# Attention and a 64-expert layer on one core: second table cleared later, a fifth raw slot, three shared tiles stored by ScalarE

## The chip, the cores and the metric

The kernel runs on one core of one Trainium2 chip. The metric is the device time of one launch in microseconds; lower is better.

## The reference

Four batches of 512 tokens by 512 features go through an attention layer and then through a layer of 64 experts, everything in float32.

```python
# attention, per batch: layer norm, keys are the given context followed by new ones
q, k_new, v_new = xn @ wq.T, xn @ wk.T, xn @ wv.T
k, v = concat([ctx, k_new]), concat([ctx, v_new])
x = x + softmax(q @ k.T / sqrt(512)) @ v @ wo.T

# experts: 64 experts, the best 6 per token, at most 128 tokens each
scores = softmax(xf @ gate_w.T);  topk_w, topk_idx = top_k(scores, 6)
gu = einsum('ech,ehi->eci', xf[buf_tok], gate_up_proj)     # hidden width 192
eo = einsum('eci,eih->ech', silu(g) * u, down_proj) * buf_w
routed = zeros.at[buf_tok].add(eo)
shared = silu(xf @ shared_gate_w.T) * (xf @ shared_up_w.T) @ shared_down_w.T   # hidden width 384
x = x + routed + shared
```

## The kernel before, in words

Every float32 product is made of three TensorE matmuls on a high and a low part of each operand (`product`, lines 1189 to 1191). ScalarE (ACT) copies an operand to its high part, and VectorE (DVE) subtracts to get the low part.

**Two stages.** `attention_and_router` works through four batches b = 0 to 3. `experts` then runs 64 experts; its first instructions are woven into the last batch. Each stage has one program per engine, and the order of the work on each is written out by hand, with counting semaphores between them.

**Attention, on SyncE (`sync`, line 337).** SyncE issues nearly all loads and stores, in one queue. Before batch 0 it loads x and the first weights, stores zeros to the padding rows of the table, of `x2_rows` and of the output (lines 406 to 408), waits for these, and then clears `second_sum`, a table of 2048 + 128 rows of 512 in HBM, from the zero rows of `x2_rows` in two DMAs (lines 411 and 413). `body(b)` then loads `ctx`, the next x and `wo`, moves part of the transposed probabilities by small DMAs (`move_pair`, half by SyncE, half by ScalarE at line 324; the tile is `pT_lo<-res` in the trace), loads the next `ctxT'`, `wq'` and `wk'`, stores eight tiles of the batch's results (`out` at line 381, `x2_rows` at line 383), keeps `x2T` and loads `wv'`. TensorE then needs the moved pieces for its transposes at line 1005 and the products behind them. GpSimd (POOL) scatters the routing table.

**Experts.** Expert n's weights, gate, up and most of down, are one load of 1 MiB into `raw[n % 4]` (line 1369); the rest of down comes for two experts at once into one of two `rest` tiles (line 1373). A raw slot is free again when VectorE has split the down part of the expert in it. Loads 0 and 1 are issued inside the last batch, load 2 when its projection is done, load 3 and the later ones when `routed` is signalled (line 774), because slot 3 lies over memory of the attention stage. ScalarE and VectorE split the weights of expert e + 3 while TensorE works on expert e.

**Adding results.** The result rows of each expert, and of 12 of the 16 tiles of the shared part, go from PSUM through ScalarE (`out_rows`, line 1530) into one of six `eo` tiles, and from there with an adding indirect DMA by GpSimd into HBM (`add_rows`, line 1442). These 76 sets are numbered r = 0 to 75; even ones add to the output, odd ones to `second_sum`, and each waits until the one two before it has landed (line 1440). Before each GpSimd may gather the rows of a later expert (line 1434). The first three sets are the shared tiles (0, 0), (0, 1) and (0, 2). The sum at the end (`merge`, line 1471) adds `second_sum` to the output; four shared tiles of batch 2 are added by VectorE and stored plainly by SyncE (line 1417).

Of the kernel before, what the change touches and what calls it, by code (L numbers as in the profile page):

```python
# [102 lines left out]
def attention_and_router(nc, ctx, sem, t, table, x2_rows, second_sum, x2T_kept, kept):  # L103
# [232 lines left out]

    def sync(sp, before_last_rows):
# [16 lines left out]
        def body(b, more):  # L354
            load_item(b, more, "ctx", b)
            if more:

                if b:
                    sp.wait_ge(chosen_ready, b)
                    sp.wait_ge(router_exp, b * 2 * NT)  # L360
                else:
                    sp.wait_ge(group_taken, place(0, "first", ("xnT", NT - 1)) + 1 + BANKS)
                for a in range(QUADS):
                    sp.dma_start(xn[a * SQ:(a + 1) * SQ, :, :], x_quads[b + 1, a]).then_inc(x_loaded, 16)
            load_item(b, more, "wo")

            move_pair(sp, b, 0, 2)
            sp.wait_ge(pair_moved, (b + 1) * 16 * QUADS * QUADS)
            sp.dma_start(res[:, :, :], x_v[b]).then_inc(res_loaded, 16)
            if more:  # L370
                load_item(b, more, "ctxT'", b + 1)
                move_xnT(sp, b, 0, 2)
                for name in ("wq'", "wk'"):
                    load_item(b, more, name, b + 1)
            if not more:
                for name in ("sg", "su", "sd"):
                    load_item(b, more, name)
                before_last_rows(sp)
            for i in range(NT):
                sp.wait_ge(base_ready, b * NT + i + 1)  # L380
                sp.dma_start(out_v[b, i], res[:, i, :]).then_inc(base_stored, 16)
                sp.wait_ge(x2_ready, b * NT + i + 1)
                sp.dma_start(x2_v[b, i], x2[:, i, :]).then_inc(x2_stored, 16)
            if more:

                sp.wait_ge(group_taken, place(b, more, ("x2T", NT - 1)) + 1 + BANKS)
                for n in range(2):
                    sp.dma_start(x2T_kept[b, n], plain(x2T[n].rearrange("p c n -> p (c n)"))
                                 ).then_inc(x2T_stored, 16)
                load_item(b, more, "wv'")  # L390
# [9 lines left out]
        for name in FIRST_ITEMS[1:]:  # L400
# [8 lines left out]
        sp.wait_ge(pads_stored, 48)  # L409
        zeros = x2_rows[T:ROWS, :]  # L410
        sp.dma_start(second_sum[0:T, :].rearrange("(n p) d -> n p d", p=P),
                     zeros.unsqueeze(0).to_broadcast([T // P, P, D])).then_inc(kept.sum_cleared, 16)
        sp.dma_start(second_sum[T:ROWS, :], zeros).then_inc(kept.sum_cleared, 16)
# [783 lines left out]
RAW = 4  # L1197
# [55 lines left out]
CHAINED = len(SETS)  # L1253
SETS += [("shared", tile) for tile in TILES_OF[LAST]]
# [12 lines left out]
def experts(nc, ctx, sem, t, table, x2_rows, second_sum, x2T_kept, kept):  # L1267
# [10 lines left out]
    rest = [sb(f"rest{n}", [P, D]) for n in range(2)]  # L1278
# [10 lines left out]
    raw.append(sb("raw3", [P, ROW]))  # L1289
# [29 lines left out]
    rest_loaded = [sem(f"rest_loaded{n}") for n in range(2)]  # L1319
# [25 lines left out]
    tiles_stored = sem("tiles_stored")  # L1345
    last_rows_added = sem("last_rows_added")
# [19 lines left out]
    def load_weights(sp, n):  # L1366
        if n >= RAW:
            sp.wait_ge(weights_split, PIECE_NO["dn", n - RAW, 0] + 1)
        sp.dma_start(raw[n % RAW][:, :], t["expert"][n], max_dma_last_dim=4096).then_inc(raw_loaded[n % RAW], 16)
        if n % 2 == 0:  # L1370
            if n >= 4:
                sp.wait_ge(weights_split, PIECE_NO["dn", n - 3, 0] + 1)
            sp.dma_start(rest[n // 2 % 2][:, :], t["rest"][n // 2]).then_inc(rest_loaded[n // 2 % 2], 16)
# [19 lines left out]
    def sync(sp):  # L1393

        sp.wait_ge(kept.group_full, kept.projected)
        load_weights(sp, 2)

# [4 lines left out]
        for n in range(3, 7):  # L1402
            load_weights(sp, n)
        for e in range(E):
            if e + 7 < E:
                load_weights(sp, e + 7)
# [16 lines left out]
    def gpsimd(pool):  # L1423
# [13 lines left out]
        def add_rows(what):  # L1437
            r = SET_NO[what]
            if r >= 2:
                pool.wait_ge(added[r % 2], r // 2 * 16)  # L1440
# [14 lines left out]
        pool.wait_ge(kept.sum_cleared, 32)  # L1455
        gather(3)
        add_rows(("shared", (0, 0)))
        for e in range(4, 7):
            gather(e)
        add_rows(("shared", (0, 1)))  # L1460
        gather(7)
        gather(8)
        add_rows(("shared", (0, 2)))
# [10 lines left out]
        for n in range(2):  # L1474
            pool.wait_ge(added[n], CHAINED // 2 * 16)
# [10 lines left out]
    def act_weights(act, first, past):  # L1486
        for kind, n, part in PIECES[first:past]:
# [3 lines left out]
            else:  # L1491
                hi, (own_rows, _) = dn[n % DN_SLOTS][0], rest_rows(n)
                act.activation(hi[:, 0:D], raw[n % RAW][:, GU:ROW], ACT.Copy)  # L1493
                act.wait_ge(rest_loaded[n // 2 % 2], n // 4 * 16 + 16)
                act.activation(hi[own_rows, D:2 * D], rest[n // 2 % 2][own_rows, :], ACT.Copy).then_inc(weights_high, 1)  # L1495
# [19 lines left out]
    def scalar(act):  # L1515
# [8 lines left out]
        def out_rows(what):  # L1524
            r = SET_NO[what]
            act.wait_ge(dn_full, r + 1)
            if r >= EO:
                act.wait_ge(added[r % 2], ((r - EO) // 2 + 1) * 16)
# [3 lines left out]
        out_rows(("shared", (0, 0)))  # L1532
        out_rows(("shared", (0, 1)))
# [10 lines left out]
        out_rows(("shared", (0, 2)))  # L1544
# [31 lines left out]
    def dve_weights(dve, first, past):  # L1576
        for kind, n, part in PIECES[first:past]:
# [4 lines left out]
            else:  # L1582
                (hi, lo), (own_rows, other_rows) = dn[n % DN_SLOTS], rest_rows(n)
                subtract(dve, lo[:, :], raw[n % RAW][:, GU:ROW], hi[:, 0:D])
                subtract(dve, hi[other_rows, D:2 * D], rest[n // 2 % 2][own_rows, :],
# [217 lines left out]
def build(nc, t):  # L1803
# [4 lines left out]
    with ExitStack() as ctx:  # L1808
# [9 lines left out]
        kept.idx_all = ctx.enter_context(nc.sbuf_tensor("idx_all", [P, E + T // P], I32))  # L1818
        kept.tab_loaded = sem("tab_loaded")
# [74 lines left out]
```

## Time and profile before

| | us |
|---|---|
| median of 3 runs | 797.64 (796.4 to 797.65) |
| the profiled execution, its own time | 801.92 |
| span of its trace | 800.2 |
| PE busy in the span | 758.1 (95%) |
| DVE, ACT, POOL busy | 604.1, 449.7, 318.5 |
| attention stage (PE never long idle) | about 0 to 400 |
| expert stage | about 400 to 771 |
| end: last tiles and sum | 771 to 800.2 |

All times below are microseconds from the start of the span. A row of the timeline shows start, duration, engine, line, operation, output and inputs, and in brackets how long the engine had been idle before it and what ended that. The DMA share is the mean share of the 16 DMA engines' time that packets took; with two queues at work it can pass 1.

### The profile page before, as it was taken

Reading aid. Unit: us, or ns where it says so; the run is one execution under the profiler, and the core shown is the slowest. Engines: PE = TensorE matmul, PEld = TensorE weight load, DVE = VectorE, ACT = ScalarE, POOL = GpSimd, SP = SyncE. Lnnn points to the kernel's source line nnn. Section 1 sums busy time; section 2 is a strip of 40 time slices with the busy share of each in tenths; the row PEclk is TensorE's granted clock in tenths of the full one; section 3 lists DMA queues with packets and bytes.
Section 4 is the critical chain, followed back from the end, with each engine's and each line's share of the span. In section 5 each row is a group of like instructions: output and inputs, shape, how many; then the busy total and the mean of one; then the engine's idle time right before and its main releaser. Section 6 shows DMA issues by size and latency. Waiting matters only on the chain.

```text
span 800.2 us, 10843 instructions
## 1 busy us (share of the span) xinstructions
PE 758.1 (95%) x3774; PEld 640.8 (80%) x3774; DVE 604.1 (75%) x1191; ACT 449.7 (56%) x795; POOL 318.5 (40%) x256
## 2 busy tenths in 40 slices
PE   6998999999999999999999999999999999998972
PEld 5886877878888787888788789998888898887752
DVE  6545575895768866785577899999999999998622
ACT  3425323253332433344153899999899898988610
POOL 1000010348104351055315556556666577555530
PEclk9999999999999999999999999999999999999997
DMA  4895435545436356343466999999999999999888
GB/s 164 292 239 142 126 138 210 131 133 159 190 126 159 107 170 242 113 95 130 169 231 179 318 349 349 350 357 354 344 356 344 350 347 355 343 352 339 212 178 190
DMA packets 84757, 188.75 MB, mean 236 GB/s; under 512 B 26000, under 2 KB 32528, under 8 KB 81040
## 3 DMA queue, kind: packets, MB, share of 16 engines
q1 hardware_dynamic: 53488, 143.41, 49.8%
q0 software_dynamic: 19056, 40.98, 22.1%
q10 hardware_dynamic: 12160, 3.67, 2.3%
q8 instruction: 31, 0.51, 0.3%
q14 instruction: 22, 0.18, 0.1%
HBM read 144.38 MB, written 43.92 MB: 235 GB/s over the span
## 4 chain that ended last, share of the span: by engine, by line
PE 59%; DMA 12%; DVE 7%; issue 6%; POOL 6%; ACT 5%; ACTq 2%; SPq 0%; POOLq 0%; DVEq 0%
PE bank L1189 9%; PE bank L1191 9%; PE bank L1190 9%; DMA raw<-expert_in 7%; PE ps_gu L1189 3%; PE scores L1189 3%; PE ps_gu L1191 3%; PE ps_gu L1190 3%; PE scores L1191 3%; PE scores L1190 3%; POOL second_sum L1442 2%; POOL out_rows L1442 2%; PE bank L1005 2%; DVE gu_lo L1574 2%; PE bank L1168 1%
## 5 line engine op out<-in xcount | busy, mean ns | idle before, releaser
L480 POOL DMA_INDIRECT table<-rows,slot x72 | 84.7, 1177 | 145.0 <-DVEq L929 112.7
L1574 DVE TENSOR_TENSOR gu_lo<-raw,gu_hi 128x768 fp32r<-128x768 f32 x126 | 120.1, 955 | 14.2 <-ACT gu_hi L1490 13.2
L1490 ACT ACTIVATE gu_hi<-raw 128x768 fp32r<-128x768 f32 x128 | 107.3, 841 | 7.4 <-DMA raw<-expert_in 7.3
L1189 PE MATMUL ps_gu<-gu_hi,xgT_hi 128*128 128x384 f32 x256 | 91.8, 358 | 0.0
L1191 PE MATMUL ps_gu<-gu_hi,xgT_lo 128*128 128x384 f32 x256 | 86.8, 339 | 0.0
L1190 PE MATMUL ps_gu<-gu_lo,xgT_hi 128*128 128x384 f32 x256 | 86.5, 338 | 0.0
L508 ACT ACTIVATE qT<-bank 128x512 fp32r<-128x512 f32 x32 | 19.1, 597 | 109.1 <-PE bank L1191 78.1
L1434 POOL DMA_INDIRECT xg<-x_rows,idx_all x39 | 46.7, 1198 | 42.2 <-DVEq L750 17.4
L1442 POOL DMA_INDIRECT out_rows<-product,idx_all x25 | 44.4, 1774 | 36.5 <-DMA out_rows<-product,idx_all 17.3
L513 ACT ACTIVATE pbuf<-scores,negmax 128x1024 f32<-128x1024 f32 x16 | 17.8, 1113 | 65.2 <-DVE negmax L679 48.4
L651 DVE TENSOR_TENSOR qT<-bank,qT 128x512 fp32r<-128x512 f32 x32 | 22.0, 688 | 41.2 <-ACT qT L508 41.2
L1190 PEld LDWEIGHTS ps_gu<-gu_lo,xgT_hi 128*128 128x128 f32 x256 | 48.6, 190 | 0.0
L1189 PEld LDWEIGHTS ps_gu<-gu_hi,xgT_hi 128*128 128x128 f32 x256 | 48.4, 189 | 0.0
L1191 PEld LDWEIGHTS ps_gu<-gu_hi,xgT_lo 128*128 128x128 f32 x256 | 48.4, 189 | 0.0
L1574 DVE TENSOR_TENSOR dn_lo<-raw,dn_hi 128x512 fp32r<-128x512 f32 x64 | 43.9, 687 | 2.5 <-ACT dn_hi L1495 1.9
L1574 DVE TENSOR_TENSOR dn_hi<-rest,dn_hi 64x512 fp32r<-64x512 f32 x64 | 43.9, 687 | 0.9
L1189 PE MATMUL bank<-xnT_hi,w_hi 128*128 128x512 f32 x112 | 44.2, 395 | 0.0
L1574 DVE TENSOR_TENSOR xgT_lo<-ps_xgT,xgT_hi 128x512 fp32r<-128x512 f32 x64 | 43.8, 684 | 0.2 <-ACT xgT_hi L1509 0.2
L1191 PE MATMUL bank<-xnT_hi,w_lo 128*128 128x512 f32 x112 | 43.7, 390 | 0.0
L1190 PE MATMUL bank<-xnT_lo,w_hi 128*128 128x512 f32 x112 | 43.6, 389 | 0.0
L1493 ACT ACTIVATE dn_hi<-raw 128x512 fp32r<-128x512 f32 x64 | 40.5, 633 | 2.7 <-DVEq L774 2.7
L644 DVE TENSOR_TENSOR w_lo<-stage,w_hi 128x2048 fp32r<-128x2048 f32 x16 | 36.5, 2289 | 7.1 <-ACT w_hi L500 7.0
(293 smaller groups left out, 2214.3 us busy)
## 6 DMA issues: line engine op xcount, KB each, us to landing
raw<-expert_in SPq DMA_DIRECT2D x64, 1024.0 KB, 13.4
rest<-rest_in SPq DMA_DIRECT2D x32, 256.0 KB, 9.9
x_rows<-pbuf SPq DMA_DIRECT2D x17, 256.0 KB, 2.1
xn<-x_in SPq DMA_DIRECT2D x16, 256.0 KB, 5.0
stage<-wkT_in SPq DMA_DIRECT2D x4, 1024.0 KB, 4.9
stage<-ctxT_in SPq DMA_DIRECT2D x4, 1024.0 KB, 7.4
stage<-wvT_in SPq DMA_DIRECT2D x4, 1024.0 KB, 9.0
stage<-ctx_in SPq DMA_DIRECT2D x4, 1024.0 KB, 10.3
```

Of the source, the lines that this page charges most:

```text
L480: pool.indirect_dma_start(out=table, out_offset=bass.IndirectOffsetOnAxis(ap=slot[:, i, k:k + 1], axis=0), in_=rows[:, i, k, :], in_offset ...
L508: act.activation(split_dest(group)[0], split_source(key, group), ACT.Copy).then_inc(high_done, 1)
L644: dve.tensor_tensor(lo, item_stage(key, name), hi.bitcast(F32), ALU.subtract).then_inc(item_low, 1)
L651: dve.tensor_tensor(lo, split_source(key, group), hi.bitcast(F32), ALU.subtract).then_inc(group_taken, 1)
L1189: pe.matmul(out, still[0], moving[0], start=first, stop=False)
L1190: pe.matmul(out, still[0], moving[1], start=False, stop=False)
L1191: return pe.matmul(out, still[1], moving[0], start=False, stop=last)
L1434: pool.indirect_dma_start(out=xg[e % XG], out_offset=None, in_=x2_rows, in_offset=index(("expert", e))).then_inc(gathered[e % XG], 16)
L1442: pool.indirect_dma_start(out=(t["out"], second_sum)[r % 2], out_offset=index(what), in_=eo[r % EO], in_offset=None, compute_op=ALU.add).t ...
L1490: act.activation(gu[n % GU_SLOTS][0][part], gate_up_of(n, part), ACT.Copy).then_inc(weights_high, 1)
L1493: act.activation(hi[:, 0:D], raw[n % RAW][:, GU:ROW], ACT.Copy)
L1574: return dve.tensor_tensor(lo, x, hi.bitcast(F32), ALU.subtract)
```

## The change

The clearing of `second_sum` leaves the start of SyncE's program. It is done in `body(1)` and `body(2)`, behind the load of `wk'`: in batch 1 the 128 padding rows and tiles 3 to 7, in batch 2 tiles 8 to 15. Tiles 0 to 2 are not cleared. Instead the first three shared tiles are stored plainly into them by ScalarE, each right behind its `out_rows`. GpSimd adds these three no more; it waits once for the three stores before its loop over the experts, and the sets from r = 3 on are chained as before. `raw` has five slots and `rest` three. The new `raw3` and `rest2` lie in memory that both stages keep, so load 3 is issued with load 2, ahead of `routed`; `raw4` takes the place of the old `raw3`. The room comes from the reserve for GpSimd's DMA descriptors, which is set to 4096 bytes per partition.

```diff
+    def clear_sum(sp, b):
+        zeros = x2_rows[T:ROWS, :]
+        if b == 1:
+            sp.wait_ge(pads_stored, 48)
+            sp.dma_start(second_sum[T:ROWS, :], zeros).then_inc(kept.sum_cleared, 16)
+        half = T // P // 2
+        first = LEAD_TILES if b == 1 else half
+        sp.dma_start(second_sum[first * P:b * half * P, :].rearrange("(n p) d -> n p d", p=P),
+                     zeros.unsqueeze(0).to_broadcast([b * half - first, P, D])).then_inc(kept.sum_cleared, 16)
...
                 for name in ("wq'", "wk'"):
                     load_item(b, more, name, b + 1)
+                if b:
+                    clear_sum(sp, b)
...
-        sp.wait_ge(pads_stored, 48)
-        zeros = x2_rows[T:ROWS, :]
-        sp.dma_start(second_sum[0:T, :].rearrange("(n p) d -> n p d", p=P),
-                     zeros.unsqueeze(0).to_broadcast([T // P, P, D])).then_inc(kept.sum_cleared, 16)
-        sp.dma_start(second_sum[T:ROWS, :], zeros).then_inc(kept.sum_cleared, 16)
...
-RAW = 4
+RAW = 5
+REST = 3
...
+def added_before(r):
+    return len(range(LEAD_TILES + (r - LEAD_TILES) % 2, r, 2)) * 16
...
-    raw.append(sb("raw3", [P, ROW]))
+    raw.append(kept.raw3)
+    raw.append(sb("raw4", [P, ROW]))
...
-            if n >= 4:
-                sp.wait_ge(weights_split, PIECE_NO["dn", n - 3, 0] + 1)
-            sp.dma_start(rest[n // 2 % 2][:, :], t["rest"][n // 2]).then_inc(rest_loaded[n // 2 % 2], 16)
+            if n >= 2 * REST:
+                sp.wait_ge(weights_split, PIECE_NO["dn", n - 2 * REST + 1, 0] + 1)
+            sp.dma_start(rest[n // 2 % REST][:, :], t["rest"][n // 2]).then_inc(rest_loaded[n // 2 % REST], 16)
...
         sp.wait_ge(kept.group_full, kept.projected)
         load_weights(sp, 2)
+        load_weights(sp, 3)
...
         sp.wait_ge(kept.routed, 1)
-        for n in range(3, 7):
+        for n in range(4, E):
             load_weights(sp, n)
-        for e in range(E):
-            if e + 7 < E:
-                load_weights(sp, e + 7)
...
-            if r >= 2:
-                pool.wait_ge(added[r % 2], r // 2 * 16)
+            if r >= LEAD_TILES + 2:
+                pool.wait_ge(added[r % 2], added_before(r))
...
-        pool.wait_ge(kept.sum_cleared, 32)
-        gather(3)
-        add_rows(("shared", (0, 0)))
-        for e in range(4, 7):
+        pool.wait_ge(kept.sum_cleared, 48)
+        for e in range(3, 9):
             gather(e)
-        add_rows(("shared", (0, 1)))
-        gather(7)
-        gather(8)
-        add_rows(("shared", (0, 2)))
+        pool.wait_ge(lead_stored, LEAD_TILES * 16)
         for e in range(E):
             gather(e + 9)
...
-        out_rows(("shared", (0, 0)))
-        out_rows(("shared", (0, 1)))
+        def lead_rows(i):
+            out_rows(("shared", (0, i)))
+            act.wait_ge(eo_ready, i + 1)
+            act.dma_start(second_sum[i * P:(i + 1) * P, :], eo[i]).then_inc(lead_stored, 16)
+
+        lead_rows(0)
+        lead_rows(1)
...
-        out_rows(("shared", (0, 2)))
+        lead_rows(2)
...
-    nc = bacc.Bacc("TRN2", target_bir_lowering=False, num_devices=1)
+    nc = bacc.Bacc("TRN2", target_bir_lowering=False, num_devices=1, dynamic_dma_scratch_size=4096)
```

## Rows read from the trace of the kernel before

**Rows 1.** The page: granted clock and DMA share, 40 slices of 20 us.
```profile
PEclk9999999999999999999999999999999999999997
DMA  4895435545436356343466999999999999999888
```

**Rows 2.** Timeline of PE: its waits for the moved pieces, batches 0 and 2.
```profile
71.40 1.58 PE L1005 MATMUL bank<-ident,pbuf 128*128 128x128 f32 x8 [3.57 <-DVE v_lo L651]
...
264.88 1.16 PE L1005 MATMUL bank<-ident,pbuf 128*128 128x128 f32 x8 [0.33 <-DVE v_lo L651]
```

**Rows 3.** Chain that ended last: start, duration, the moved pieces landing, batches 0 and 2.
```profile
60.58 6.16 DMA pT_lo<-res
...
256.58 3.65 DMA pT_lo<-res
```

**Rows 4.** DMA issues of 31 to 37 us: queue, count, KB each, us to landing.
```profile
stage<-ctx_in SPq DMA_DIRECT2D x1, 1024.0 KB, 19.1
...
second_sum<-x_rows SPq DMA_DIRECT2D x1, 15.7
```

**Rows 5.** Windows: length, busy PE, PEld, DVE, ACT, POOL, granted clock, DMA share, GB/s.
```profile
32.00:55.00 23.00, 23.00 (x104) 19.02 (x103) 9.56 (x12) 6.11 (x9) 0.00 (x0) 1.00 0.97 282
...
70.00:75.00 5.00, 3.60 (x14) 3.03 (x15) 4.40 (x8) 3.19 (x7) 0.00 (x0) 0.70 0.80 321
```

**Rows 6.** Timeline of SP, batch 1: the load ahead of the new clears, the one behind.
```profile
192.83 0.33 SPq L352 DMA_DIRECT2D stage<-wkT_in  x1
...
216.10 0.93 SPq L352 DMA_DIRECT2D stage<-wvT_in  x1
```

**Rows 7.** Timeline of ACT, batch 1: the use of that load.
```profile
225.11 1.92 ACT L500 ACTIVATE w_hi<-stage 128x2048 fp32r<-128x2048 f32 x1 [5.25 <-DMA stage<-wvT_in]
```

**Rows 8.** Timelines of DVE and PE, batch 1: the routing sums, PE's product behind them.
```profile
239.35 1.00 DVE L900 TENSOR_TENSOR earlier<-earlier,xn 128x64 bf16<-128x64 bf16 x4
...
241.37 0.20 PE L1143 MATMUL bank<-chosen_b,before 128*128 128x64 bf16 x1
```

**Rows 9.** Windows of the expert stage, columns as in the fifth group.
```profile
480.00:540.00 60.00, 60.00 (x337) 54.15 (x336) 58.88 (x104) 55.42 (x104) 35.13 (x27) 1.00 1.06 352
540.00:735.00 195.00, 188.76 (x1031) 166.74 (x1030) 180.72 (x319) 175.76 (x326) 123.18 (x81) 0.99 1.06 348
```

**Rows 10.** DMA issues of 480 to 540 us.
```profile
raw<-expert_in SPq DMA_DIRECT2D x13, 1024.0 KB, 12.8
...
out_rows<-product,idx_all POOLq DMA_INDIRECT x4, 8.3
```

**Rows 11.** DMA issues of 600 to 660 us.
```profile
raw<-expert_in SPq DMA_DIRECT2D x12, 1024.0 KB, 13.8
...
out_rows<-product,idx_all POOLq DMA_INDIRECT x5, 8.8
```

**Rows 12.** Timeline of POOL: adds r = 3, 23, 70, 75, and the first load behind.
```profile
453.39 1.58 POOL L1442 DMA_INDIRECT second_sum<-eo,idx_all  x1 [0.30 <-issue]
...
545.62 1.78 POOL L1442 DMA_INDIRECT second_sum<-eo_above,idx_all  x1 [2.20 <-DMA second_sum<-eo,idx_all]
...
753.50 1.55 POOL L1442 DMA_INDIRECT out_rows<-product,idx_all  x1 [2.11 <-DMA out_rows<-eo,idx_all]
...
765.96 1.55 POOL L1442 DMA_INDIRECT second_sum<-eo,idx_all  x1 [0.79 <-DMA second_sum<-product,idx_all]
771.58 0.86 POOL L1478 DMA_DIRECT2D raw<-second_sum  x1 [4.07 <-DMA second_sum<-eo,idx_all]
```

**Rows 13.** Timeline of ACT: where the three stores go, and the last result tile.
```profile
437.44 0.33 ACT L1522 ACTIVATE silu<-ps_gu 128x192 f32<-128x192 f32 x1 [1.51 <-PE ps_gu L1191]
...
447.57 0.60 ACT L1530 ACTIVATE eo<-ps_dn 128x512 f32<-128x512 f32 x1 [0.24 <-PE ps_dn L1191]
...
755.99 0.69 ACT L1530 ACTIVATE eo<-ps_dn,tab 128x512 f32<-128x512 f32 x1 [1.57 <-PE ps_dn L1752]
```

**Rows 14.** Chain that ended last: start and duration of one DMA issue on ACT.
```profile
58.57 0.64 ACTq L324
```

More of the change, by code:

```diff
@@ L1277, in experts @@
     raw = [sb(f"raw{n}", [P, ROW]) for n in range(2)]
-    rest = [sb(f"rest{n}", [P, D]) for n in range(2)]
+    rest = [sb(f"rest{n}", [P, D]) for n in range(2)] + [kept.rest2]
     gu = [(halves(sb("gu_hi0", [P, GU], F32R)), halves(sb("gu_lo0", [P, GU], F32R)))]
@@ L1318, in experts @@
     raw_loaded = [sem(f"raw_loaded{n}") for n in range(RAW)]
-    rest_loaded = [sem(f"rest_loaded{n}") for n in range(2)]
+    rest_loaded = [sem(f"rest_loaded{n}") for n in range(REST)]
     gathered = [sem(f"gathered{n}") for n in range(XG)]
@@ L1345, in experts @@
     tiles_stored = sem("tiles_stored")
+    lead_stored = sem("lead_stored")
     last_rows_added = sem("last_rows_added")
@@ L1474, in gpsimd @@
         for n in range(2):
-            pool.wait_ge(added[n], CHAINED // 2 * 16)
+            pool.wait_ge(added[n], added_before(CHAINED + n))
         pool.nop().then_inc(chains_done, 1)
@@ L1493, in act_weights @@
                 act.activation(hi[:, 0:D], raw[n % RAW][:, GU:ROW], ACT.Copy)
-                act.wait_ge(rest_loaded[n // 2 % 2], n // 4 * 16 + 16)
-                act.activation(hi[own_rows, D:2 * D], rest[n // 2 % 2][own_rows, :], ACT.Copy).then_inc(weights_high, 1)
+                act.wait_ge(rest_loaded[n // 2 % REST], n // 2 // REST * 16 + 16)
+                act.activation(hi[own_rows, D:2 * D], rest[n // 2 % REST][own_rows, :], ACT.Copy).then_inc(weights_high, 1)
     def act_silu(act, n):
@@ L1526, in out_rows @@
             act.wait_ge(dn_full, r + 1)
-            if r >= EO:
-                act.wait_ge(added[r % 2], ((r - EO) // 2 + 1) * 16)
+            if r >= EO + LEAD_TILES:
+                act.wait_ge(added[r % 2], added_before(r - EO + 2))
+            elif r >= EO:
+                act.wait_ge(lead_stored, LEAD_TILES * 16)
             scale = tab[:, what[1], 1:2] if what[0] == "expert" else 1.0
             act.activation(eo[r % EO], ps_dn[:, r % 2, :], ACT.Copy, scale=scale).then_inc(eo_ready, 1)
-        out_rows(("shared", (0, 0)))
-        out_rows(("shared", (0, 1)))
+        def lead_rows(i):
[4 more added lines that the diff above has]
+        lead_rows(1)
         gate(0)
@@ L1584, in dve_weights @@
                 subtract(dve, lo[:, :], raw[n % RAW][:, GU:ROW], hi[:, 0:D])
-                subtract(dve, hi[other_rows, D:2 * D], rest[n // 2 % 2][own_rows, :],
+                subtract(dve, hi[other_rows, D:2 * D], rest[n // 2 % REST][own_rows, :],
                          hi[own_rows, D:2 * D]).then_inc(weights_split, 1)
@@ L1818, in build @@
         kept.idx_all = ctx.enter_context(nc.sbuf_tensor("idx_all", [P, E + T // P], I32))
+        kept.raw3 = ctx.enter_context(nc.sbuf_tensor("raw3", [P, ROW], F32))
+        kept.rest2 = ctx.enter_context(nc.sbuf_tensor("rest2", [P, D], F32))
         kept.tab_loaded = sem("tab_loaded")
```

## The prediction

> **What bounds the kernel now.** I read the slices of the page first [rows 1]. The DMA share has two full stretches, 20 to 60 us and everything from 440 us on; between them the DMA engines are half idle. Up to 440 us TensorE (PE) runs nearly without a gap, so that stage costs what its matmuls cost, plus PE's few waits. The longest by far is in batch 0: 3.57 us before the transposes at 71.40. The same transposes in batch 2 waited 0.33 us [rows 2]. In both the chain of waits runs through the small moves `pT_lo<-res`: behind ScalarE's last issue they took 6.16 us in batch 0 and 3.65 us in batch 2 [rows 3]. The work is the same; what differs is the queue. The clearing DMA took 15.7 us to land, and the `ctx` load behind it 19.1 us [rows 4]. [...]
>
> The expert stage has three limits close together. From 480 to 540 us PE is busy 60.00 of 60.00 us and DVE 58.88; from 540 to 735 us PE is busy 188.76 of 195, so 6.24 us are idle [rows 9]. The DMA share is 1.06 and the rate 348 to 352 GB/s in both. The third limit is the chain of adds. Add r = 23 starts at 545.62 and r = 70 at 753.50, 47 steps of 4.42 us; each waits for the add two before it. After the loads, r = 70 to 75 take 5 steps of 2.49 us [rows 12]. The last result tile is started at 755.99 and ready at 756.68 [rows 13], yet its add goes out at 765.96, 9.3 us later. So at the end the adds are last, not the matmuls and not the loads. At 771.58 the final sum begins; the 28.6 us from there to the end of the span are not changed.
>
> **The change part by part.**
>
> *Clear taken out of the start.* It removes 17 tiles of 256 KiB, 4.46 MB. At 282 GB/s [rows 5] that is 15.8 us, which agrees with the landing of 15.7 us [rows 4]. With `ctx`, x and `wo` (3.15 MB) the queue holds 7.6 MB from 32 us on, 27 us of work, so it is full until about 59 us, when the moves are being issued. Without the clear it is empty after 11 us, near 43 us. Then batch 0 should look like batch 2: PE waits 0.33 instead of 3.57 us, a gain of 3.24 us. The lower bound is the difference of the moves alone, 2.51 us [rows 3]. [...] All of this is on PE's path, and PE has no slack behind it until 440 us, so it reaches the expert stage whole. Sum: -4.7 us (-2.5 to -4.7).
>
> *Clear put into batches 1 and 2.* It goes behind the `wk'` load, near 193 us in batch 1 [rows 6]; the queue is half idle there [rows 1]. Queued behind it on SyncE's ring are eight stores of results, the two of `x2T` and the `wv'` load at 216.10. Spread over all engines the larger part, 8 tiles or 2.1 MB, takes 7.4 us at 282 GB/s and is over before 216. Then it costs nothing. If it lasts longer, `wv'` lands late. ScalarE already waits 5.25 us for it [rows 7]; behind it DVE finishes the routing sums at 240.35, 1.0 us before PE's product that needs them [rows 8]. The upper bound is that the new clear takes as long as the old one, 15.7 us [rows 4]: from about 198 to 213.7 us, then 2.1 MB of stores, 7.4 us, so the two of `x2T` and `wv'` run some 5.5 us late, and less the 1.0 us PE waits 4.5 us in each of two batches. I take 0.3 us (0 to +9), near the lower end, because 2.1 MB at the rate used above are done before 216.
>
> What the rows show of spreading is one DMA of 16 tiles in 15.7 us [rows 4]. [...]
>
> *Fifth raw slot, third rest slot.* Load 3, 1.05 MB, moves from 441 us to near 402 us, where the DMA share is 0.6 [rows 1], so it is hidden. It is gone from the full stretch: 1.05 MB at 348 GB/s, 3.0 us. Every later load is issued one expert earlier. That can fill PE's 6.24 idle us [rows 9], but this is worth nothing while the adds are last. What remains is that the loads end 3.0 us earlier, and that the adds go from 4.42 to 2.49 us a step 3.0 us earlier: 3.0 x (1 - 2.49 / 4.42) = 1.3 us. Bounds: 0, and all of the 6.2 us. I take -1.3.
>
> *Three adds less, three stores more.* Two stores are issued by ScalarE before the `silu` at 437.44, which waited 1.51 us for PE [rows 13]; an issue is 0.64 us [rows 14], 1.28 for both, so they are covered. The third comes behind `out_rows` at 447.57, where ScalarE is otherwise full: 0.64 us, part of it on the path. GpSimd waits for its landing before `gather(9)` and the add r = 3. Landing as an add did, 8.3 us [rows 10], from 448.8, that is 457; then a gather, so r = 3 goes out near 458.5 instead of 453.39 [rows 12]. Queued behind are the later gathers (needed six experts later, no cost) and the chain. From r = 3 to 23 the steps were 4.61 us; the chain can do 4.42, so 20 steps regain 3.8 of the 5.1 us, and all of it if landings are shorter there. What is left at r = 23 is 0 to 1.3 us. Both items together: +0.4 us (0 to +2).
>
> *Smaller descriptor reserve.* At no time are more than a few DMAs of GpSimd open (two adds, up to five gathers), so I cost it at nothing; GpSimd's issue durations of 1.55 to 1.78 us [rows 12] would show it.
>
> Sum: -4.7 + 0.3 - 1.3 + 0.4 = -5.3 us. The profiled execution took 801.92 us with a span of 800.2, 4.3 us above the median of 797.64. Nothing in the sum scales with that, so the profiled time becomes 796.6 and the median 792.3 us.
>
> **The rivals.**
>
> 1. *The loads were the limit after all.* If the adds speed up once ScalarE and the loads no longer collide with them, the whole 6.2 us of PE's idle time go instead of 1.3: 797.64 - 4.7 + 0.3 + 0.4 - 6.2 = 787.4 us. For it: PE has no idle time at all up to 540 us and 6.24 us after it. Against it: the 9.3 us by which the adds trail. Chance 0.12.
>
> 2. *The moved clears hold `wv'` up.* If one engine copies one tile, five or eight tiles take as long as sixteen did, and the stores and `wv'` wait in the same rings. Half of the 5.5 us, less the 1.0 us, is 1.8 us in each of two batches: +3.6 instead of +0.3, 795.6 us. For it: everything of the batch's end is queued behind the clear. Against it: the 5.25 us of ScalarE's wait are hidden today, and part of DVE's work behind has gaps. Chance 0.18. [...]
>
> 3. *Slower: the deeper load queue lengthens the adds.* With five slots SyncE has one more load open all the time. Between 480 to 540 and 600 to 660 us the landing of loads rose from 12.8 to 13.8 us and that of the adds from 8.3 to 8.8 [rows 10, 11]: more open loads, slower adds. Another open load (about +4.4 us of landing) could add several times as much. Each us of landing is 0.5 us a step; over 52 adds from r = 23 it takes +0.27 us of landing to eat up 7 us, which turns -5.3 into +1.7. With the +0.5 us that the rows show once more, the price is 52 x 0.25 = 13 us, 805.3 us; with half of it, 798.8 us, which I give as its time. Against it: when adds are late, the six result tiles run out, ScalarE stops and with it the loads, so the queue empties again. Chance 0.10.
>
> 4. *The clear did not cause the wait of batch 0.* The x load shares the queue too. Then only the fifth slot gains: 797.64 + 0.3 - 1.3 + 0.4 = 797.0 us. Against it: 3.15 MB are 11 us of work, gone long before the moves. Chance 0.06.
>
> **How the numbers follow.** The forecast, 792.3 us, has 0.54, with a range of its own of 789.5 to 795. Below it lies rival 1, above it rivals 2, 4 and 3. The range from 786.5 to 798 takes in rivals 1, 2 and 4, and leaves out rival 3 and the far ends of 2. About 0.2% (1.6 us) is what a measurement of this kernel can tell from no change, so faster means below 796.0: the forecast, rival 1 and two thirds of rival 2, 0.78. Same: rival 4 and most of what is left of rival 2, 0.11. Slower: rival 3 and its like, 0.11.
>
> **What would show it.** In the trace after: PE's wait before the transposes of batch 0 near 0.3 us and a full clock behind it; the first wait for `routed` about 5 us earlier, near 436 us; ScalarE's waits for expert loads gone; the steps of the adds still about 4.4 us while loads run, and the last add about 5 us earlier, near 760.5. The landing of `wv'` in batches 1 and 2 against 9 us decides rival 2, that of the adds rival 3. The prediction is wrong if the adds' landing moves by more than 0.3 us either way, since 52 of them stand in one chain.

## The result, and the profile after

The changed kernel takes 804.68 us (median of 7 runs, 802.0 to 805.72), the kernel before 797.65 beside it. The ratio is 1.0068, 95% interval 1.0041 to 1.0095: slower, where 792.3 us was forecast. The profiled execution of the changed kernel took 802.37 us, with a span of 800.5. It lies 2.3 us under its median and that of the kernel before 4.3 us over its own, so the two traces end almost together (0.3 us apart in their spans) where the medians are 7.0 us apart; what the change costs as a whole is read from the medians, and where it costs from the traces.

The page, granted clock and DMA share, answers to [rows 1]. The windows (columns as in [rows 5] and [rows 9]) show batch 0's wait and the same stage of batches 1 and 2:

```profile
PEclk9999999999899999999999999999999999999997
DMA  5833552636536375524295899999999999999888
...
60.00:80.00 20.00, 19.85 (x94) 16.03 (x94) 18.03 (x32) 9.61 (x17) 1.02 (x1) 1.00 0.33 112
200.00:220.00 20.00, 15.72 (x67) 12.35 (x66) 12.13 (x21) 6.59 (x9) 2.75 (x4) 0.83 0.50 193
300.00:320.00 20.00, 16.03 (x70) 12.75 (x70) 12.10 (x21) 5.88 (x8) 2.74 (x4) 0.91 0.52 205
```

The first window is what was forecast: where PE waited 3.57 us [rows 2] and ran at a clock of 0.70 [rows 5], it is busy 19.85 of 20 us at full clock. The other two are new. PE is busy only 15.72 and 16.03 us, at a granted clock of 0.83 and 0.91: it was 0.50 from 208 to 214 us in batch 1 and from 314 to 316 us in batch 2. PE's timeline in batch 1 has two waits ahead of the transposes of x2, which stretch from 207.77 us on:

```profile
207.77 1.09 PE L1013 MATMUL bank<-ident,pbuf 128*128 128x128 f32 x4 [1.83 <-DVEq L852]
...
211.09 1.94 PE L1013 MATMUL bank<-ident,pbuf 128*128 128x128 f32 x8 [2.23 <-DVE qT L659]
```

The waits of 190 to 225 us say who was late (us in total, times, longest), and the chain of waits through the same stretch (start, duration, what) gives the order:

```profile
POOL rstd L474 <- DMA table<-rows,slot: 11.4, 1, 11.4
DVE pbuf L794 <- POOL rstd L474: 6.6, 2, 6.1
...
190.94 12.17 DMA table<-rows,slot
203.28 0.58 POOL rstd L474
203.89 0.55 DVE pbuf L794
204.44 0.67 DVE res L849
```

GpSimd's last scatter of batch 0's routing table was issued at 190.94 us and landed 12.17 us later. GpSimd waits for all scatters before it goes on to the norms (`rstd`) of batch 1; VectorE waits 6.1 us for the first norm, and PE for VectorE's `pbuf`. In the kernel before, GpSimd has no wait for scatters there at all, only for VectorE:

```profile
POOL rstd L466 <- DVE veps L848: 6.3, 4, 1.7
```

What lay in the way is the moved clear. The packet records of the changed kernel show 20 packets of 64 KiB in batch 1 (five tiles, on five engines, 191.9 to 202.2 us) and 32 in batch 2 (on eight engines, 293.2 to 303.8 us): five and eight at a time, four times behind each other, 2.42 to 3.00 us each. The last scatter landed at 203.1 us, 0.9 us after the last of them had gone. In batch 2 GpSimd waited 10.6 us. The same records show how a few bytes come to wait so long. The packets of GpSimd's queue (64 bytes or less) take 0.013 us each in the median; in batch 1 exactly five of them start at 194.42 to 194.92 us, five at 196.85 to 197.34 and five at 199.27 to 199.76, each time where the five large ones change over, and the rest from 201.70 on. Batch 2 shows the same with eight (295.88 to 296.28, 298.36 to 298.70, 300.78 to 301.12). So in both batches each busy engine started one small packet between two of its large ones, 15 in batch 1 and 24 in batch 2 over the three changeovers, and the scatters' last packets followed as the large ones ended.

**The ledger.** PE issues the same 3774 matmuls in the same order in every kernel here, so the start of the same matmul can be compared. Rows are points of the program (start in the kernel before), columns the difference to that kernel in us. The labels are those of the experiments below. All columns stand against one execution of the kernel before, the one that took 4.3 us more than its median. e4 ran on a chip that no other column here is from, where e1 to e4 all show further short waits of 1.0 to 1.6 us (near 165, 194, 292 and 362 us, in e4 some 8 us later) that the other chips don't; of its column only the steps from row to row are used, not the level.

```
before   after  e4      e6     e9     e12    e8     e11    e10
 67.4    -1.0   -0.0    +0.5   -0.1   +0.5   -1.3   +0.3   -0.4   ahead of batch 0's wait
 77.7    -5.8   +2.7    -4.3   -4.9   -4.4   -6.2   -4.4   -5.1   behind it
199.1    -6.4   +5.8    -4.8   -5.3   -5.1   -6.7   -4.9   -5.6   batch 1, ahead of the norms
225.7    +0.0   +5.8    -4.8   -5.3   -4.9   -6.7   -4.9   -5.6   behind them
318.7    +5.7   +7.5    -4.7   -5.3   -4.8   -6.5   -5.0   -5.5   batch 2, behind the norms
421.0    +5.3  +11.3    -4.7   -5.4   -5.1   -6.9   -5.6   -5.5   last batch
459.6    +5.3   +9.7    -6.3   -7.0   -6.8   -8.4   -7.2   -7.2   experts begin
588.1    +4.1   +8.5    -7.5   -8.3   -7.9   -7.2   -8.4   -8.4
661.9    +3.3   +7.6    -8.3   -8.9   -8.8   -5.9   -9.3   -8.1
750.9    +2.1   +8.2    -8.3   -7.8  -10.2   -6.2   -8.3   -8.0
```

The changed kernel wins 4.8 us at batch 0's wait and loses 6.4 and 5.7 us behind the norms of batches 1 and 2. e5, the changed kernel once more, loses 6.7 and 6.6 us at the same two places (-5.3 at 199.1, +1.4 at 225.7, +8.0 at 318.7). In the expert stage the profiled execution regains 3.2 us, and ScalarE's waits for expert loads, 7.3 us before, are down to 0.7. The 3.2 us are no steady gain: e5 has none of these waits either and stands at +7.8 at 459.6, +5.9 at 661.9 and +8.8 at 750.9. The adds hold the end as before [rows 12], now at

```profile
L1500 ACT ACTIVATE gu_hi<-raw 128x768 fp32r<-128x768 f32 x128 | 107.3, 841 | 0.7 <-DMA raw<-expert_in 0.7
...
460.14 1.63 POOL L1457 DMA_INDIRECT second_sum<-eo,idx_all  x1 [0.30 <-issue]
...
550.60 1.98 POOL L1457 DMA_INDIRECT second_sum<-eo_above,idx_all  x1 [2.00 <-DMA second_sum<-eo,idx_all]
...
755.37 1.55 POOL L1457 DMA_INDIRECT out_rows<-product,idx_all  x1 [1.23 <-DMA out_rows<-eo,idx_all]
...
767.81 1.55 POOL L1457 DMA_INDIRECT second_sum<-eo,idx_all  x1 [0.53 <-DMA second_sum<-product,idx_all]
773.51 0.87 POOL L1488 DMA_DIRECT2D raw<-second_sum  x1 [4.15 <-DMA second_sum<-eo,idx_all]
```

(the first row is ScalarE's group of weight copies: busy, mean ns, and at its end the idle time before them; the others are the adds r = 3, 23, 70 and 75 and the load behind).

From that last load to the end of the span it was 28.6 us before and is 27.0 now. Nearly all of the difference is in one instruction, with which GpSimd ends its program (in the kernel before and in the changed one: line, instruction, count, duration in ns as least/median/most, start):

```profile
L1823 POOLq DRAIN  x1: 2602/2602/2602, 797.4 to 797.4; - x1
```

```profile
L1842 POOLq DRAIN  x1: 1173/1173/1173, 799.1 to 799.1; - x1
```

It takes 2602 ns in the kernel before and in e8, and 1173 ns in all twelve traces with the reserve of 4096 bytes. So 1.43 us of the span go with the change. The reserve is the part of the change that all twelve have and these two lack, next to the place of the new tiles in memory; no run changes it alone, so it is the likely cause and not a shown one.

### The profile page after: what moved, and what is told of

Same layout as the page of the kernel before. It is cut to its first block, busy times and chain, and to the rows that moved or that the text cites. A ratio compares the mean times of both kernels' runs of the same rounds, so it can differ in the third digit from the quotient of the medians.

```text
span 800.5 us, 10842 instructions
## 1 busy us (share of the span) xinstructions
PE 758.5 (95%) x3774; PEld 640.1 (80%) x3774; DVE 603.6 (75%) x1191; ACT 449.4 (56%) x795; POOL 310.1 (39%) x253
## 4 chain that ended last, share of the span: by engine, by line
PE 69%; DMA 10%; DVE 6%; POOL 5%; issue 5%; ACT 3%; SPq 1%; POOLq 0%; DVEq 0%
PE bank L1197 9%; PE bank L1199 9%; PE bank L1198 9%; PE ps_gu L1197 4%; PE ps_gu L1199 4%; PE ps_gu L1198 4%; PE scores L1197 3%; PE scores L1199 3%; PE scores L1198 3%; DMA table<-rows,slot 3%; PE ps_dn L1197 2%; PE ps_dn L1199 2%; PE ps_dn L1198 2%; PE ps_xgT L1727 2%; DMA out_rows<-product,idx_all 2%
## 5 line engine op out<-in xcount | busy, mean ns | idle before, releaser
L1591 DVE TENSOR_TENSOR gu_lo<-raw,gu_hi 128x768 fp32r<-128x768 f32 x126 | 120.2, 955 | 11.4 <-ACT gu_hi L1500 10.4
L1457 POOL DMA_INDIRECT out_rows<-product,idx_all x24 | 41.0, 1707 | 27.4 <-DMA out_rows<-product,idx_all 14.9
```

Source lines behind the costliest of these rows:

```text
L1457: pool.indirect_dma_start(out=(t["out"], second_sum)[r % 2], out_offset=index(what), in_=eo[r % EO], in_offset=None, compute_op=ALU.add).t ...
L1591: return dve.tensor_tensor(lo, x, hi.bitcast(F32), ALU.subtract)
```

## The experiments

The experiments went to three chips; the kernel before took 807.85, 798.74 and 797.61 us (medians) beside the first four, the next four and the last four. So all is compared by the ratio to the kernel before on the same chip.

**Is it the clears, and what about them?** e1 writes the same bytes with the 128 rows of a tile outermost, in packets of 2 KiB, by its records mostly 15 to 17 at a time while the clear runs:

```diff
-        sp.dma_start(second_sum[...].rearrange("(n p) d -> n p d", p=P),
-                     zeros.unsqueeze(0).to_broadcast([b * half - first, P, D]))
+        sp.dma_start(second_sum[...].rearrange("(p n) d -> p n d", p=P),
+                     zeros.unsqueeze(1).to_broadcast([P, b * half - first, D]))
```

> The changed kernel, with each clear of the second table laid out over 128 partitions' worth of rows (outermost dimension 128, rows of 2 KB) instead of 5 or 8 whole tiles. Theory H (held scatters): GpSimd's table scatters share DMA engines with packets of 64 KiB, each of about 2.4 us; GpSimd waits for all of them before it may compute the next norms, and so TensorE waits in batches 1 and 2 and its clock falls. Then the last scatter lands within about 3 us, both waits (6.4 and 5.7 us with the clock) are gone: 804.7 - 12 = 792.7 us. Rival S (stores and wv' late behind the clear): the bytes are the same and the queue is the same, so at most the part from the five and eight busy engines goes; little change, 803 to 805 us. Rival M (memory traffic of the clears slows everything around it): no change, 804.7 us.

Measured: 800.41 us, ratio 0.9903 (0.988 to 0.9925). GpSimd's wait is 4.6 us in batch 1 and 5.8 in batch 2 (theory H had the last scatter land within 3 us), and PE's waits ahead of the transposes of x2 are down to 0.2 us. Spreading changed two things at once, the engines and the packets. e2 leaves the shape and only limits the packets:

```diff
-                     zeros.unsqueeze(0).to_broadcast([b * half - first, P, D]))
+                     zeros.unsqueeze(0).to_broadcast([b * half - first, P, D]), max_dma_last_dim=512)
```

> The changed kernel with the clears still over 5 and 8 whole tiles, but cut into packets of 2 KB instead of 64 KiB. H with packet size as the cause: a scatter waits for one small packet at a time, the waits in batches 1 and 2 go as with the spread layout, 793 us. H with the few engines as the cause (what counts is that five or eight engines are busy for 10 us): the waits stay, 804.7 us. S: 804.7 us, since the clears hold the same rings for as long.

Measured: 799.09 us, ratio 0.9884 (0.9862 to 0.9907), GpSimd's wait 4.5 us. The limit counts bytes here: the packets are 512 bytes long, not the 2 KiB that the expectations say of this and of the later kernels with the limit. The queue's row of the page (packets, MB, share) has 6604 more than the changed kernel, 13 tiles in 512 bytes less the 52 large ones. By the records most of the time five to seven of them are under way together in batch 1 (193.6 to 205.9 us) and eight to twelve in batch 2 (290.1 to 302.7 us), against 15 to 17 in e1. So a clear on few engines did no harm by itself. The short packets have a price of their own, though it is hidden: SyncE's next store is held at its issue for 5.50 us in e2 and 7.50 in e9, against 0.34 to 0.35 in the changed kernel, e1 and e12, and PE does not wait longer for that. e9 is the same kernel on the third chip (0.9914); these are the changed kernel's row and its own:

```profile
q1 hardware_dynamic: 53473, 142.62, 49.2%
```

```profile
q1 hardware_dynamic: 60077, 142.62, 50.0%
```

e12 goes the other way: long packets, but on all 16 engines.

```diff
-        sp.dma_start(second_sum[...].rearrange("(n p) d -> n p d", p=P),
-                     zeros.unsqueeze(0).to_broadcast([b * half - first, P, D]))
+        count = (b * half - first) * P // 16
+        sp.dma_start(second_sum[...].rearrange("(p m) d -> p (m d)", p=16),
+                     zeros[0:count, :].rearrange("m d -> (m d)").unsqueeze(0).to_broadcast([16, count * D]))
```

> The changed kernel with each moved clear written as 16 long rows (80 KiB in batch 1, 128 KiB in batch 2), so that all 16 DMA engines take part with packets as large as before. Theory Q (a large packet ahead in a DMA engine holds GpSimd's small scatters by its own length, and the number of packets in each engine decides: four each in the changed kernel, one or two here): GpSimd's wait for the table's scatters 6 to 9 us, less than 1.5 us of waiting by TensorE in batches 1 and 2 together, ratio 0.992 to 0.998. Theory S (any packet of such size costs the same stop, whatever the number): GpSimd's wait stays at 10 to 12 us and the ratio at 1.003 to 1.008. Theory O (even so, the spread takes the harm away entirely): wait under 5.5 us, ratio as e9.

Measured: 790.28 us, ratio 0.9912 (0.9889 to 0.9935). By its records the rows were cut in two, 32 packets of 40 KiB in batch 1 and 32 of 64 KiB in batch 2, 16 at a time and so two on each engine, one of 64 KiB 2.42 to 2.84 us. GpSimd's and VectorE's waits, first batch 1, then batch 2 (windows 190 to 225 and 290 to 325 us):

```profile
POOL rstd L476 <- DMA table<-rows,slot: 6.3, 1, 6.3
...
DVE pbuf L796 <- POOL rstd L476: 1.6, 2, 1.2
...
POOL rstd L476 <- DMA table<-rows,slot: 6.6, 1, 6.6
```

In batch 2 packets of exactly the changed kernel's size hold the scatters for 6.6 us when two stand on an engine and 10.6 us when four do; the difference, 4.0 us, is a little less than two packets of 2.42 us. This is theory Q. PE keeps its pace: its longest wait between 190 and 330 us is 0.4 us, so the norms had room for these 6.3 us. That the ratio is better than the forecast for Q fits this room.

**Is GpSimd's wait the whole path?** e3 and e6 leave the clears as they are and put the norms ahead of the wait.

```diff
             pool.tensor_tensor(rstd2[:, i:i + 1], ...).then_inc(rstd_ready, 1)
         if not more:
             return
+        if b:
+            pool.wait_ge(scattered, b * 16 * NT * K)
+            pool.sem_inc(slots_free, 1)
...
-        pool.wait_ge(scattered, (b + 1) * 16 * NT * K)
-        pool.sem_inc(slots_free, 1)
+        if b == B - 2:
+            pool.wait_ge(scattered, (b + 1) * 16 * NT * K)
+            pool.sem_inc(slots_free, 1)
```

This is e6. e3 had no exception for the last of these waits.

> The changed kernel with its clears untouched; only GpSimd's wait for its 24 scatters of a batch is moved behind the four norms of the next batch. H: the scatters still take about 12 us, but the norms no longer wait for them; both waits of TensorE go, 792.7 us. S and M: nothing that they name is changed, 804.7 us.

Measured: 812.38 us, ratio 1.0044 (1.0025 to 1.0063), a miss. The two waits were gone, but a new one came in the last batch (PE's timeline):

```profile
410.36 0.76 PE L1198 MATMUL ps_gu<-v_hi,kT_hi 128*128 128x512 f32 x1 [10.41 <-DMA v_lo<-x2T_kept]
```

SyncE waits on `slots_free` before it loads the table and then `x2T`; the edit made that signal late. With the exception:

> The changed kernel with its clears untouched (64 KiB packets on 5 and 8 engines in batches 1 and 2), but GpSimd computes the next batch's norms before it waits for the scatters of batches 0 and 1; for batch 2, whose scatters the last batch's gathers need, the wait stays where it was. Theory H (held scatters: all that the moved clears cost is GpSimd's wait ahead of the norms): ratio about 0.989 (0.986 to 0.992), no wait of TensorE over 1.2 us between 190 and 330 us, and no 10 us wait near 410 us. Rival C (the clears also take bandwidth from what TensorE, ScalarE or VectorE wait for): some of the 1.8% stays, ratio 0.994 to 1.002, and waits for loads in batches 1 and 2 are seen in the trace.

Measured: 792.34 us, ratio 0.9925 (0.9899 to 0.9951), beside 1.0077 (1.0046 to 1.0107) for the changed kernel on the same chip:

> The changed kernel itself, on the chip of the runs of this call, as the measure for the others. Every theory: ratio to the kernel before 1.007 (1.003 to 1.010), GpSimd's rstd waiting 11 to 12 us for the table's scatters in batch 1 and 10 to 11 in batch 2.

The waits of 190 to 225 us show that GpSimd now waits for VectorE only, as in the kernel before:

```profile
POOL rstd L474 <- DVE veps L860: 8.8, 4, 4.0
```

From 199 to 319 us the ledger of e6 stands still (-4.8 to -4.7), with the large packets in the queues. So the two waits behind the norms cost 1.5% (about 12 us), and the clears cost PE nothing besides. Rival C falls. The medians of e5 and e6, 805.34 and 792.34 us, are 13.0 us apart, beside the 6.7 and 6.6 us that e5 lost at the two places.

**What is each part worth?** e8 is the kernel before with the clear moved and nothing else, in 512-byte packets.

> The kernel before with one thing changed: the clear of the second table goes out in batches 1 and 2 in 2 KiB packets and not at the start; four slots, GpSimd's adding scatters for the shared tiles. Theory S (the parts add up: slots and stores alone gave 0.56%, clear, slots and stores together 1.16%): ratio 0.994 (0.992 to 0.996), the 5 us won in batch 0 still there at the end. Theory P (the adds and loads of the experts' part soak up what the start gave): ratio 0.997 to 1.000, TensorE 5 to 6 us ahead at 400 us and less than 2 at 760. Theory L (slots and stores are worth nothing, once the clear is out of the way): 0.988 to 0.990.

Measured: 795.76 us, ratio 0.9969 (0.9946 to 0.9992). In the ledger 8.4 us are won by 460 us and 5.9 left at 662. The group of weight copies points to where it went:

```profile
L1499 ACT ACTIVATE gu_hi<-raw 128x768 fp32r<-128x768 f32 x128 | 107.3, 841 | 13.8 <-DMA raw<-expert_in 13.6
```

ScalarE's waits for loads grew from some 7 to 13.6 us: an expert stage that starts earlier, with four slots and the full DMA stretch unchanged, waits for its loads. The ratio is the one that theory P gives; the ledger of the profiled execution, with 6.2 us left at 751 us, is nearer to theory S. The medians (-3.0 us) leave less than that execution shows. Part of it is the slow execution that the ledger stands against (4.3 us over its median), part that this one took 794.59 us, 1.2 under its own. e4 does the opposite: slots and stores, but the 13 tiles cleared at the start.

> The changed kernel with the clear back at the start of SyncE's program (13 tiles and the padding rows), so fifth slot, third rest slot and ScalarE's stores alone. H: the waits of batches 1 and 2 go (-12 us) and that of batch 0 comes back (+4.8 us), and the expert stage keeps its gain of about 3 us: 797 us, a little under the kernel before (797.6 - 3 = 795). If the expert stage's gain was only the later start and not the slots: 797.6 us or more. S and M: the same as H here, since they too blame the clears of batches 1 and 2.

Measured: 803.99 us, ratio 0.9944 (0.9916 to 0.9971), better than H's 797 us (a ratio of 0.999). Batch 0's wait is back, longer than in [rows 2] (PE's timeline):

```profile
73.08 1.94 PE L1005 MATMUL bank<-ident,pbuf 128*128 128x128 f32 x8 [5.27 <-DVE v_lo L651]
```

e9, e10 and e11 take the slot and the stores apart, all with 512-byte clears. e10 (and e7 before it) has `RAW = 4` and `REST = 2`; e11 keeps five slots and gives the three shared tiles back to GpSimd.

```diff
-            act.wait_ge(eo_ready, i + 1)
-            act.dma_start(second_sum[i * P:(i + 1) * P, :], eo[i]).then_inc(lead_stored, 16)
...
-        for e in range(3, 9):
-            gather(e)
-        pool.wait_ge(lead_stored, LEAD_TILES * 16)
+        gather(3)
+        add_rows(("shared", (0, 0)))
...
```

> Clears in 2 KiB packets as in the second kernel of the first call, with four raw slots and two rest slots in place of five and three; the stores by ScalarE stay. Theory U (the fifth slot has a use, since ScalarE waited 7.3 us for loads with four): ratio 0.991 to 0.994, ScalarE's wait for raw loads back at 5 to 8 us. Theory N (the slot is hidden: TensorE and the adds end the kernel, ScalarE's waits for loads are slack): ratio 0.988 to 0.990 like with five slots, ScalarE's wait for loads back all the same. If four slots come out below 0.987, the deeper queue costs something by itself.

Measured: 792.86 us, ratio 0.993 (0.9907 to 0.9953), with 1.3 us of waiting for loads, not the 5 to 8 of theory U. e2 had been on another chip, so the comparison was made again on one:

> The changed kernel with the two moved clears in 2 KiB packets (e2_small again), now on one chip with its own four-slot and no-stores forms. Theory U (the fifth slot has a use of its own): ratio to the kernel before 0.989, 0.3% or more below e10. Theory N (the slot's work is hidden; e2 and e7 differed because they ran on two chips): ratio 0.991 to 0.993, within 0.2% of e10.

> The same with four raw slots and two rest slots (e7_small_four again). Both theories: ratio 0.993 (0.991 to 0.995), ScalarE's wait for raw loads 1 to 2 us.

> The changed kernel with its clears in 2 KiB packets and its five slots, but the first three shared tiles go by GpSimd's adding scatters as in the kernel before. Theory T (the stores carry the gain in the experts' part: with four slots, TensorE was 2.6 us further ahead at 588 us with stores than without, and ScalarE waited 1 us for loads and not 14): ratio 0.996 to 0.998, like e8, and ScalarE's waits for loads 5 us or more even with five slots. Theory D (slot or stores, either one removes ScalarE's waits for loads, and one is enough): ratio 0.990 to 0.993, within 0.2% of e9, waits for loads under 3 us.

Measured: e9 790.44 us, 0.9914 (0.9892 to 0.9937); e10 792.17 us, 0.9933 (0.9908 to 0.9958); e11 791.93 us, 0.9938 (0.9913 to 0.9962). The idle time of ScalarE's weight copies in e9, e10 and e11:

```profile
L1501 ACT ACTIVATE gu_hi<-raw 128x768 fp32r<-128x768 f32 x128 | 107.3, 841 | 0.0
```

```profile
L1501 ACT ACTIVATE gu_hi<-raw 128x768 fp32r<-128x768 f32 x128 | 107.2, 840 | 6.2 <-DMA raw<-expert_in 6.0
```

```profile
L1506 ACT ACTIVATE gu_hi<-raw 128x768 fp32r<-128x768 f32 x128 | 107.3, 841 | 3.4 <-DMA raw<-expert_in 3.3
```

The slot is worth 1.7 us and the stores 1.5 us by the medians. Both are small against the noise: the intervals overlap, and run against run five of e9's six times lie below all six of e11's, but only three of them below all of e10's. e9 against e10 is 0.19%, which is what theory N named; e10's 6.2 us of waits for loads are more than the 1 to 2 that both theories had. e11 lies just outside D on both counts (0.24% from e9, 3.4 us of waits) and farther from T.

Together (e9 at 0.9914 against e8 at 0.9969, two chips) it is 0.55% or 4.4 us, and e4 against the kernel before says the same, 0.56%. Both pairs hold the 1.43 us of GpSimd's last instruction too, so slot and stores have about 3.0 us of it, near 1.7 + 1.5.

The lowest times of this study are e12 and e9 (790.28 and 790.44 us); by the ratio e2, which is e9 on another chip, is lowest at 0.9884. All of them beat the kernel before and the changed one.

## Why the prediction was wrong

**Clear taken out of the start: right.** Forecast -4.7 us, measured -4.8 at the same place (67.4 to 77.7 in the ledger). Of the forecast, 3.24 us are the wait, and 1.5 us stand for the clock, 0.30 of the 5 us of [rows 5]; that share was the author's estimate, and no run shows it by itself. What the traces show is a clock of 0.50 from 72 to 75 us in the kernel before and of 1.00 there in the changed one. The wait and the lower clock behind it are gone, and with the clear back at the start (e4) the wait is back too. Rival 4 falls. About 1 us more stands ahead of it in the profiled pair (-1.0), but it differs from kernel to kernel with nothing changed there (-1.3 to +0.5) and is not put down to the change. What was too simple is that these 4.7 us go into the sum whole: e8, with this part alone and no harm in batches 1 and 2, has 0.9969, 2.5 us (0.6 to 4.3), and its ledger gives part of the gain back in the expert stage, where ScalarE waits 13.6 us for loads.

**Clear put into batches 1 and 2: the step that failed.** Forecast +0.3 us (0 to +9), measured +6.4 and +5.7, 12.1 us in all. The step named what is queued on SyncE behind the clear, the stores and `wv'`, and stopped there. It asked how long the clear lasts, and the upper bound even gave it the old 15.7 us, but not what else shares the DMA engines in that time. The last of GpSimd's 24 scatters of the batch before are on them, out of another queue (128 packets, started from 191.2 to 202.3 us in batch 1), and what stands behind them was to be found in the kernel: GpSimd waits for all of them and only then computes the norms that VectorE and PE need next. That wait is the missing term. Four large packets per engine (2.42 us each, 9.7 us) bound it from the trace after; what PE lost was less, because the norms had some room (5.2 us of such waiting in e9 cost nothing). The upper bound of the range, +9, also had a slip: 213.7 + 7.4 is 5.0 us past 216.1, not 5.5.

**Rival 2** had the layout right and the victim wrong. The large clears took 10.3 and 10.6 us, not the old one's time. `wv'` landed 9.0 us after its issue, as in the kernel before (DMA issues of 199 to 221 us: queue, count, KB, us to landing):

```profile
stage<-wvT_in SPq DMA_DIRECT2D x1, 1024.0 KB, 9.0
```

e6 shows that it was not issued late either: with the large packets in the queues and only the norms moved it goes out at 211.34 us, 4.8 us before the 216.10 of [rows 6], which is all that this kernel is ahead by then.

```profile
211.34 0.91 SPq L363 DMA_DIRECT2D stage<-wvT_in  x1
```

That one engine copies one tile fits the trace, five and eight large packets at a time. By itself this cost nothing: e2 keeps the shape and is among the fastest (0.9884). The harm came with the large packets: at each changeover of five or eight of them five or eight small ones start, and in e12, with two large packets on an engine (of 40 KiB in batch 1) in place of four, GpSimd waits 6.3 and 6.6 us for the scatters and not 11.4 and 10.6.

**Fifth slot: the size about right, the reason only in part.** Forecast -1.3 us, measured -1.7 (e9 against e10) with an uncertainty of the same size. ScalarE's waits for loads went, as forecast; that the loads end 3.0 us earlier and the adds speed up for it was not measured by itself.

**Stores for adds: probably the wrong sign.** Forecast +0.4 us, measured -1.5 by the medians, not certain. The first add (r = 3 at 460.14) came less late than forecast, which was 458.5, or 463.8 with the 5.3 us by which everything was late there. That three adds less make room in the full DMA stretch fits ScalarE's waits for loads (3.4 us in e11, none in e9), but isn't shown beyond that.

**Smaller reserve: a term put at nothing.** GpSimd's issues are as long as before (72 scatters at 1.18 us each in both), as the prediction said. But it also held the 28.6 us at the end for unchanged, and they are 27.0: 1.43 us less in GpSimd's last instruction.

**Rival 1 and rival 3.** The adds' steps from r = 23 to 70 became (755.37 - 550.60) / 47 = 4.36 us, from 4.42, and the landing of the group in [rows 11] went from 8.8 us to 8.4. That is past the 0.3 us that the prediction named as a sign of being wrong, but the other four groups of adds in that window moved by -0.4 to +0.2 and the same group has 8.9 in e9, so it is scatter and no deeper queue lengthened the chain. Loads land later, 16.0 us from 600 to 660 us instead of 13.8 (+2.2, where rival 3 had +4.4), and no harm is seen, since they are issued earlier. The last add came 9.0 us after its result tile, as before (6.6 in e9, 9.1 in e10), and PE's waits from 455 to 750 us are 6.5 us after 8.0 before (8.3 in e9), so rival 1's gain did not come either. The DMA issues of 600 to 660 us:

```profile
raw<-expert_in SPq DMA_DIRECT2D x12, 1024.0 KB, 16.0
...
out_rows<-product,idx_all POOLq DMA_INDIRECT x6, 8.4
```

**The sum.** Without the 12.1 us of the two waits the changed kernel's 804.68 us would be 792.6, and e9, the change as meant, has 0.9914 against the forecast's 792.3 / 797.64 = 0.9933. So near a hit is in part luck. Of e9's 6.9 us the clear has 2.5 and not 4.4 (-4.7 + 0.3), slot and stores 3.0 and not 0.9, and the end 1.4 and not 0: the first was forecast too high, the others too low. These shares hold for the parts added in this order, the clear first.

**Open.** All repaired kernels of the ledger gain a further 1.5 to 1.7 us between 421 and 460 us, because a stretch at a granted clock of 0.50 that the kernel before and the changed one have at 424 to 427 and 430 to 433 us is missing (3.4 us by the clock's records, so 1.7 us of full clock). e4 lacks it too, with its wait in batch 0, and e1, which is repaired, has it (426 to 430 us) and gains nothing there, so it isn't tied to the repair; what decides it wasn't found.

## What to carry to other kernels

When a transfer is moved, list not only what is queued behind it on its own queue but every transfer of other queues that is under way on the DMA engines in the same time, and who waits for the last of those. The filler transfer between two memory regions was safest here in short packets: 512 bytes or 2 KiB cost PE nothing, four of 64 KiB behind each other on an engine cost it some 6 us each time (6.4 and 5.7). Of the two, 2 KiB with 15 to 17 under way at a time (e1) also left SyncE's next issue at 0.34 us, where 512 bytes in the shape of the changed kernel held it for 4.5 to 8.0. And a wait that only protects a buffer should stand behind the work that others need, but look for who else reads its signal (e3). Last, a forecast that comes out near once one step is repaired may still have wrong parts that cancel: price them one by one.

## What the hardware showed

A packet of 64 KiB from HBM to HBM took 2.42 to 3.00 us in the changed kernel, and one small packet of another queue started between two of them on a busy engine. GpSimd's small scatters from that queue were held for longer when more of these stood on an engine: GpSimd waited 10.6 us for them behind four (batch 2) and 6.6 us behind two (e12), and in batch 1, behind four, the last took 12.17 us to land. The granted clock was 0.50 from 208 to 214 us in the changed kernel, behind waits of 1.83 and 2.23 us, and 0.83 over 200 to 220 us, while PE in e9, with waits of at most 0.3 us there, kept 1.00. In e1, with single waits of 1.54 us at 164.8 and 1.27 at 194.4, the clock was 1.00 from 160 to 200 us. In batch 1 PE lost 6.4 us in all, some 4 of them as waits and the rest, by estimate, as clock.
